# The last stage's adapters fetched by a register address in steps over six sequences, and the causal mask of two head groups by POOL

## The reference, cut to what matters

```python
# L1 attention, one of 4 layers; layer 0 is the same without rel
scores = (einsum('bhqd,bhkd->bhqk', q, k) + rel) * HEAD_DIM ** (-0.5)   # 16 heads of 8
mask = jnp.arange(S)[None, :] > jnp.arange(S)[:, None]
scores = jnp.where(mask[None, None], NEG, scores)
p = jax.nn.softmax(scores, axis=-1)
# L3_ffn: one adapter of eight for each sequence
base = jnp.einsum('btd,od->bto', x, base_W) + base_b
m1, m2 = x.mean(axis=1), (x * x).mean(axis=1)
losses = (m2 . inv_var - 2.0 * m1 . (disc_mu * inv_var) + sum(disc_mu ** 2 * inv_var)) / D
idx = jnp.argmin(losses, axis=0)
h = jax.nn.relu(x @ down_W[idx] + down_b[idx])
a = h @ up_W[idx] + up_b[idx]
return base + (a @ conv_W[idx].T + conv_b[idx])
```

## Time and profile before

| what | value |
|---|---|
| median of 3 runs | 7136.94 us (7130.81 to 7144.48) |
| the profiled execution's own time | 7138.57 us |
| its span in the trace | 7136.8 us |
| PE busy | 6011.8 us (84%) |
| DVE busy | 4420.2 us (62%) |
| ACT busy | 2803.8 us (39%) |
| POOL busy | 1534.3 us (21%) |

### The profile page before, as it was taken

The page is one execution under the profiler, slowest core; times in us unless marked ns, Lnnn a source line. Parts: engine busy times, 40 slices in busy tenths (PEclk is TensorE's granted clock), DMA queues, the critical chain, the costliest instruction groups (busy, mean ns, idle before and its releaser), DMA issues. The chain is left out here.

```text
span 7136.8 us, 123309 instructions
## 1 busy us (share of the span) xinstructions
PE 6011.8 (84%) x39533; PEld 3728.4 (52%) x39533; DVE 4420.2 (62%) x10235; ACT 2803.8 (39%) x4536; POOL 1534.3 (21%) x1885
## 2 busy tenths in 40 slices
PE   8997999999949998899879987998898987355455
PEld 5773444444426774577457754775454663234322
DVE  6764666666646763677356745774454666796565
ACT  4552222222214554355435543554444553123211
POOL 4320000000023331333133313331001224222100
PEclk9998999999969999999989998999888998678755
DMA  4333323223325540555045513552000000000000
GB/s 131 104 82 104 97 96 96 97 96 96 97 65 138 145 122 6 142 141 144 8 124 135 144 35 97 139 143 58 4 0 3 0 4 0 3 0 2 7 0 24
DMA packets 524294, 522.62 MB, mean 73 GB/s; under 512 B 56244, under 2 KB 434691, under 8 KB 501766
## 3 DMA queue, kind: packets, MB, share of 16 engines
q1 hardware_dynamic: 523990, 518.91, 26.2%
HBM read 333.65 MB, written 185.07 MB: 73 GB/s over the span
## 5 line engine op out<-in xcount | busy, mean ns | idle before, releaser
L346 DVE TENSOR_REDUCE a_mx<-a_unit 128x2 f32<-128x512 f32 (+1 forms) x1920 | 1305.0, 690 | 748.1 <-PE a_unit L522 737.9
L436 ACT ACTIVATE a_prob<-a_slot 128x1536 f32<-128x1536 f32 x640 | 928.4, 1451 | 853.3 <-PE a_slot L545 853.3
L520 PE MATMUL a_unit<-a_sk,a_sq 96*128 96x256 bf16 (+3 forms) x5120 | 752.0, 250 | 75.6 <-DMA a_sk<-a_kscratch 56.1
L1125 ACT ACTIVATE f_silu<-f_pG 128x512 f32<-128x512 f32 x528 | 314.8, 598 | 940.9 <-PE f_pG L1198 940.7
L1071 DVE TENSOR_TENSOR f_gated<-f_spread,f_silu 128x512 f32<-128x512 f32 x512 | 354.6, 693 | 403.8 <-ACT f_silu L1125 358.7
L522 PE MATMUL a_unit<-a_maskq,identb 128*128 128x256 bf16 (+1 forms) x1920 | 603.6, 314 | 0.0
L520 PEld LDWEIGHTS a_unit<-a_sk,a_sq 96*128 96x128 bf16 (+1 forms) x5120 | 399.8, 99 | 341.8 <-DVE a_mx L346 129.5
L1177 PE MATMUL f_pO<-f_hidden,f_wd 128*128 128x512 f32 x1056 | 547.1, 600 | 16.6 <-DVE f_hidden L1073 15.9
L1198 PE MATMUL f_pG<-f_xnT,f_wg 128*128 128x512 f32 x1056 | 542.7, 596 | 0.0
L1202 PE MATMUL f_pU<-f_xnT,f_wu 128*128 128x512 f32 x1056 | 541.0, 594 | 0.0
L538 PE MATMUL a_slot<-a_sq,a_sk 98*128 98x256 bf16 (+1 forms) x2560 | 463.1, 274 | 81.3 <-DMA a_sq<-a_mscratch 71.5
(11 more groups left out here) (411 smaller groups left out, 11509.8 us busy)
## 6 DMA issues: line engine op xcount, KB each, us to landing
f_spread<-f_scratch SPq DMA_DIRECT2D x1024, 128.0 KB, 2.9
a_sq<-a_qscratch SPq DMA_DIRECT2D x128, 768.0 KB, 5.7
a_sk<-a_kscratch SPq DMA_DIRECT2D x160, 384.0 KB, 6.7
a_qscratch<-a_parts SPq DMA_DIRECT2D x288, 192.0 KB, 2.2
a_qscratch<-a_parts SPq DMA_DIRECT2D x288, 128.0 KB, 2.2
a_kscratch<-a_parts SPq DMA_DIRECT2D x160, 192.0 KB, 2.2
a_kscratch<-a_parts SPq DMA_DIRECT2D x160, 128.0 KB, 2.1
a_qscratch<-a_parts SPq DMA_DIRECT2D x288, 64.0 KB, 1.8
```

Of the source, the lines that this page charges most:

```text
L346: v.tensor_reduce(dst, src, op=ALU.max, axis=AX.X, negate=True).then_inc(red_done, 1)
L436: act.activation(prob[gr % 2][:, :], slot[:, :], ACT.Exp, scale=SCALE).then_inc(exp_done, 1)
L520: pe.matmul(bank[:, at * wide:(at + 1) * wide], q, sk[b][0:KM, gr * GH + h, 0:wide], start=(at == 0), stop=False)
```

## The change

Two edits, in different stages.

*In the attention*, groups 0 and 1 of four (`SELECTED = 2`) leave out the three products with `maskk`. Instead POOL sets the exponentials to zero where a key lies behind its query, with two `affine_select` instructions on `prob` (128 x 512 float32 each) for each group. `values` of these groups waits for POOL (`sel_done`) instead of ACT. On POOL's queue group 0's pair stands ahead of 1/sqrt(var), group 1's behind it and ahead of the split of q and k.

*In the adapters*, the stage is written anew in the steps of `fours`: in step n, the stats are for sequence n+5, the normalised rows and their transpose for n+4, the losses and the choice for n+3, the first products for n+1, the last for n, the add to x for n-1. The choice is read into a register of SP, and one transfer fetches that adapter (128 x 323) from DRAM into one of four tiles. Mean and 1/std come from POOL in the steps, and there is no `row_moments`, no `every` and no `pB`. ACT sums both x and its square as it copies. `store_out` goes: SP stores each sequence two steps after its last products.

```diff
                 def step(i, j):
                     n = i * 4 + j
+                    def causal(gr):
+                        if not is_seq(n):
+                            return
+                        g.wait_ge(exp_done, n * GROUPS + gr + 1)
+                        g.sem_inc(apart, 1)
+                        wide = prob[gr % 2][:, 0:2 * BLK].rearrange("p (h q) -> p h q", q=SEQ)[:, :, 0:P]
+                        tail = prob[gr % 2][:, 2 * BLK:3 * BLK].rearrange("p (h q) -> p h q", q=P)
+                        g.affine_select(wide, wide, [[0, GH], [1, P]], ALU.is_ge, zero, base=0, channel_multiplier=-1)
+                        g.affine_select(tail, tail, [[0, GH], [1, P]], ALU.is_ge, zero, base=0, channel_multiplier=-1
+                                        ).then_inc(sel_done, 1)
                     if not rel and is_seq(n - 1):
 ...
                         g.tensor_tensor(guard[:, :, :], zeros[:, :, :], zeros[:, :, :], op=ALU.add).then_inc(guard_done, 1)
+                    causal(0)
                     if is_seq(n + 5):
                         g.wait_ge(stats_done, n + 6)
                         ln_rstd(g, chain, moments, veps, mhalf, rstd, eps, rstd_done, apart)
+                    causal(1)
 ...
-                            pe.matmul(bank.rearrange("p (h k) -> p h k", k=SEQ)[:, :, 0:P], identb,
-                                      maskk[:, :].unsqueeze(1).broadcast_to((P, 2, P)), start=False, stop=True)
+                            if gr >= SELECTED:
+                                pe.matmul(bank.rearrange("p (h k) -> p h k", k=SEQ)[:, :, 0:P], identb,
+                                          maskk[:, :].unsqueeze(1).broadcast_to((P, 2, P)), start=False, stop=True)
 ...
-                        pe.wait_ge(exp_done, m * GROUPS + gr + 1)
+                        if gr < SELECTED:
+                            pe.wait_ge(sel_done, m * SELECTED + gr + 1)
+                        else:
+                            pe.wait_ge(exp_done, m * GROUPS + gr + 1)
 ...
 # adapters: the queue of SP
+                    if is_seq(n + 3):
+                        b = (j + 3) % 4
+                        sp.wait_ge(picked, n + 4)
+                        choice = sp.value_load(at[b][0:1, 0:1], min_val=0, max_val=E - 1)
+                        if is_seq(n - 1):
+                            sp.wait_ge(yT_done, n)
+                        sp.dma_start(mine[b][:, :], w["every"][bass.ds(choice, 1), :, :].rearrange("e p c -> p (e c)")
+                                     ).then_inc(loaded[b], 16)
+                    if is_seq(n - 2):
+                        sp.wait_ge(x_done, n - 1)
+                        sp.dma_start(out[bass.ds(n - 2, 1), :, :].rearrange("s (t p) d -> p (s t) d", p=P),
+                                     rows(core["x"], (n - 2) * QT, QT)).then_inc(put, 16)
 ...
 # DVE
+                    if is_seq(n + 4):
+                        v.wait_ge(rstd_done, n + 5)
+                        ln_apply(v, rows(core["x"], (n + 4) * QT, QT), moments, rstd, xn).then_inc(xn_done, 1)
+                    if is_seq(n + 3):
+                        v.wait_ge(l_pe, n + 4)
+                        link(v.tensor_scalar(gain[:, :], pL[0:1, 0:E], -1.0 / (D * SEQ), None, ALU.mult))
+                        link(v.max(best[:, :], gain[:, :]))
+                        v.max_index(at[(j + 3) % 4][:, :], best[:, :], gain[:, :]).then_inc(picked, 1)
+                    if is_seq(n - 1):
+                        v.wait_ge(r_pe, n)
+                        v.tensor_tensor(dst, pR[:, 0:SEQ].rearrange("p (t d) -> p t d", d=D), dst, op=ALU.add
+                                        ).then_inc(x_done, 1)
+                    v.drain()
+                    if is_seq(n + 5):
+                        ln_stats(v, chain, rows(core["x"], (n + 5) * QT, QT), stats, moments, stats_done)
```

More of the change, by code:

```diff
@@ new lines, in adapters @@
+        stats = k.sb("stats", [P, QT, 6]); moments = k.sb("moments", [P, QT, 2])
+        veps = k.sb("veps", [P, QT]); rstd = k.sb("rstd", [P, QT])
+        xn = k.sb("xn", [P, QT, D]); xnT = [k.sb(f"xnT{b}", [P, SEQ]) for b in range(4)]; sqr = k.sb("sqr", [P, SEQ])
+        sum1 = k.sb("sum1", [P, 1]); sum2 = k.sb("sum2", [P, 1])
+        gain = k.sb("gain", [1, E]); best = k.sb("best", [1, E])
+        at = [k.sb(f"at{b}", [1, E], mybir.dt.uint32) for b in range(4)]
+        mine = [k.sb(f"mine{b}", [P, W]) for b in range(4)]; outb = [k.sb(f"outb{b}", [P, 1]) for b in range(4)]
@@ L2148, in adapters, with used @@
+        loaded = [k.sem(f"loaded{b}") for b in range(4)]
+        W_IN = 16 * 4
+        def used(i, j, ahead):
+            return 16 * i + ((j + ahead) // 4 + 1) * 16
         with nc.Block() as block:
@@ L2150, in _ @@
             def _(sp):
[L2151 to L2155, removed]
-                                 (sigma[:, :], w["sigma"]), (iota[:, :], core["iota8"])):
-                    sp.dma_start(dst, src).then_inc(w_in, 16)
+                for dst, src in ((mu, w["mu"]), (sigma, w["sigma"]), (base, w["base"]), (baseb, w["baseb"])):
+                    sp.dma_start(dst[:, :], src).then_inc(w_in, 16)
@@ L2159, in _ @@
+                fours(sp, step)
+                sp.wait_ge(x_done, SEQS)
+                sp.dma_start(out[SEQS - 1:SEQS, :, :].rearrange("s (t p) d -> p (s t) d", p=P),
+                             rows(core["x"], (SEQS - 1) * QT, QT)).then_inc(put, 16)
+                sp.wait_ge(put, 16 * SEQS)
             @block.gpsimd
             def _(g):
-                g.memset(every[:, :, :], 0.0).then_inc(setup, 1)
-                g.memset(biases[:, :, :], 0.0).then_inc(setup, 1)
-                g.memset(ones1[:, :], 1.0).then_inc(setup, 1)
@@ L2164, in _, with step @@
-                g.memset(onescol[:, :], 1.0).then_inc(setup, 1)
+                chain = Chain(g)
+                g.memset(length[:, :], float(SEQ)).then_inc(setup, 1)
+                chain.link(g.memset(mhalf[:, :], -0.5))
+                g.wait_ge(w_in, W_IN)
+                def step(i, j):
+                    n = i * 4 + j
+                    if is_seq(n + 1):
+                        b = (j + 1) % 4
+                        g.wait_ge(loaded[b], used(i, j, 1))
+                        if is_seq(n - 3):
+                            g.wait_ge(yT_done, n - 2)
+                        g.tensor_tensor(outb[b][:, :], mine[b][:, BC:BC + 1], baseb[:, :], op=ALU.add).then_inc(outb_done, 1)
+                    if is_seq(n + 5):
+                        g.wait_ge(stats_done, n + 6)
+                        ln_rstd(g, chain, moments, veps, mhalf, rstd, 1e-5, rstd_done, apart)
@@ L2166, in _ @@
+                fours(g, step)
             @block.vector
@@ L2234, in step @@
                                        ).then_inc(aT_done, 1)
-                        act.wait_ge(y_pe, n + 1)
-                        act.activation(yT[:, :], pY[:, 0:SEQ], ACT.Identity, bias=outb[:, 0:1]).then_inc(yT_done, 1)
-                rounds(act, step, SEQS)
+                fours(act, step)
             @block.tensor
@@ L2431, in twos @@
         step(n // 2, n % 2)
+SELECTED = 2
 def part_of(a, prefix):
@@ L2490, in load_core @@
     return core
-def store_out(nc, store, out):
-    put = nc.alloc_semaphore("out_written")
-    with nc.Block() as block:
-        @block.sync
-        def _(sp):
-            for c in range(8):
-                sp.dma_start(out.rearrange("s (t p) d -> p (s t) d", p=P)[:, c * 8:(c + 1) * 8, :],
-                             store[:, c * 8:(c + 1) * 8, :]).then_inc(put, 16)
-            sp.wait_ge(put, 128)
 def constants():
```

241 lines of the change are left out of this document (120 added, 121 removed).

## The result

| what | before | changed |
|---|---|---|
| median | 7136.94 us (7130.81 to 7144.48) | 6752.74 us (6751.02 to 6756.28, 4 runs) |
| span of the profiled execution | 7136.8 us | 6754.2 us |

The ratio is 0.9462 [0.9445, 0.9478]: 384 us less, where 321 were forecast.

The account below looks back on a forecast made before the run. Bounds: a chain through the pick in the adapters, PE in layer 0, a loop of two steps in L1. Savings 271 + 9 + 41 = 321 us from 7138.6, less 1.6 for the median: 6816 us, range 6765 to 6885.

Parts of the forecast that it names:

- The last stage: Adapters: DVE's loop with POOL bounds a step, taken as 4.8 us; stage 456 to 185 us, 271 less.
- the dear end: Adapters: upper bound of 5.9 us a step, with PE at the lower clock.
- The fetch: Adapters: three steps must hold 5 us and the fetch; even at 13.73 us, a step would be 6.2.
- Layer 0: Attention: PE saves 0.88 us a step, late transposes cost 0.6, leaving 0.28 a step, 9 us.
- the charge for DVE's standstill: L1: DVE standing still beside POOL's selects adds 0.25 us to the loop of two steps (bounds 0 and 0.8).
- The loop of two steps: L1: three legs sum to 33.67 us per two steps; only the first gains, 0.44 a step before the charge.
- The selects: POOL, attention: 0.61 us a select, 1.35 a pair with its gap, 2.47 kept for the range; nothing late at 1.35.
- all: Rival, attention: DVE gets ahead of POOL everywhere, masks bring 84 us, not 50; with adapters at 4.6, 6776; chance 0.13.
- The adapters did not stay at the lower clock: Denies a rival: adapters at lower clock or waiting for the fetch, 5.9 to 6.2 a step, 6862 us; chance 0.08.
- The masks bring nothing: Rival, attention: dear selects or L372 late; L1 gains 0.04, layer 0 loses 0.3; total 6871; chance 0.22.
- slower: Rival, attention: POOL becomes the limit if a select reaches 2.1 us; at 3 us, 7439 us; chance 0.05.

Follow-up runs that it names:

- e4: Changed kernel with DVE's stats of n+5 in the last stage moved right behind the normalised rows of n+4: 6738.4 us, ratio 0.945.
- e1: Changed kernel with all four groups masked by PE again, so the new adapters alone: 6822.3 us, ratio 0.956 to the kernel before.
- e9: Changed kernel without its selects, so groups 0 and 1 have no mask at all: 6760.2 us, ratio 0.9477.
- e3: Changed kernel with POOL's first pair of selects also waiting until DVE has split the negated maxima: 6744.1 us, ratio 0.9457.
- four masked kernels: The changed kernel and three runs with the same attention code in L1; L1 took 2671 us in their mean.
- e10: Changed kernel with all four groups left without mask, neither selects nor PE's masks: 6719.9 us, ratio 0.9421.
- e2: Kernel before with POOL's masks for two groups and the old adapters kept: 7064.7 us, ratio 0.9905.
- e6: Changed kernel with L1's row of maxima loaded ahead of the two stacks of q and k: 6749.3 us, ratio 0.9459.

## Why the prediction was right or wrong, step by step

- **The last stage: mechanism right, size wrong; this is the step that put the time outside the range.** The failed term is 31 x 4.8 = 149 us for the steps: it measured 113.8 from the first add to the last. A steady step took 3.96 us, which makes 26 of the 35 us; the other 9 are the last five steps, which take 1.9 to 2.6 us each and which the term counted as full. The filling with barrier and loads took 24.5 us in place of 32, the last store 4.6 in place of 4. That is 42 us together. By the two spans, which lie 383 us apart, 62 us were missed: these 42 and 29 of L1, less 3 of layer 0 and 6 of stages that no edit touches. The 4.8 was a value between 4.4, which is stage_a3's step and has more DVE work, and 5.9, PE at the lower clock. The loop itself is 2.65 us on DVE and 1.31 through POOL, and the second number was in the prediction (1.32); I took a neighbour's total in place of adding up the parts. And PE was granted 1.00 in all of the steps (the filling ahead of them had 0.58), so the dear end did not exist. The range allowed for nothing under 4.4 a step. e4 shows that the loop is the bound.
- **The fetch**: it landed 2.3 us after its issue (median of 27). No engine waited for it in the steady steps, as forecast; POOL's bias sum (`outb`) did so in three of the last steps, 6.6 us together.
- **Layer 0: the charge was right, the saving too large, and the total near by luck.** 0.88 saved less 0.6 for the late transposes was to give 0.28 a step, 9 us. The step went from 15.65 to 15.55 us, 0.10, and layer 0's own copies (first to last) lie 3 us closer. The stretch is 6.8 us shorter (the mean of before and e1 against four kernels with the changed attention) because 1.7 come from the filling of L1, which has masks too, and some 2 from the experts. The charge measured 0.59 in e9, and e3 names its place. But the saving was 0.69 and not 0.88: PE comes earlier to `maxima(2)` and now waits there for DVE's reduction of an earlier unit. From the first transpose of `xn` to that product lie 0.25 us before and 0.44 in the changed kernel, e3 and e9 (means of 16 steps). First before, then the changed kernel:
```profile
303.60 0.41 PE L588 MATMUL a_ring<-ident,a_xn 128*128 128x128 f32 x2
303.85 0.38 PE L520 MATMUL a_unit<-a_sk,a_sq 80*128 80x256 bf16 x2
```
```profile
304.51 0.69 DVE L362 TENSOR_REDUCE a_mx<-a_unit 128x4 f32<-128x512 f32 x1 [0.18 <-issue]
...
304.86 0.41 PE L611 MATMUL a_ring<-ident,a_xn 128*128 128x128 f32 x2
305.26 0.39 PE L536 MATMUL a_unit<-a_sk,a_sq 80*128 80x256 bf16 x2
```
- **L1: the charge for DVE's standstill was wrong.** I added 0.25 us to the loop of two steps, 16 us in all. The loop's first leg fell by 0.90, all of PE's masks, though L387 and L388 do stand still there too (0.71 and 0.54 us at 2393.07 and 2393.86, the first beside the split's L342, the second beside a select): the transposes came 3.54 us behind `scores(0)`, as they should without the masks, and their wait for DVE is 6.8 us over all of L1. e3, which removes the standstill beside the selects, leaves L1 as it was. Of the 28 us missed in L1 (by the means of above) the charge is 16. Another 9 are the last four steps of each layer: together they are 3.9 us shorter (52.4 us in the mean of before and e1, 48.5 in the four masked kernels, from copy to copy), where I had counted 0.44 each. The last 3 are the steady steps, with 0.47 in place of 0.44, which is within L1's scatter.
- **The loop of two steps: right as far as the change goes, wrong beyond it.** It forecast 0.44 a step and 0.47 came (16.93 us in the mean of before and e1, 16.46 in the four masked kernels, in the middle steps of all layers by the start of `scores(0)`). But its rule, half of PE's saving, fails in e10. No kernel here has L1 under 2659 us. That the clock is the cause of the 17 to 19 us by which e9 and e10 are longer is argued from the sums above and not shown by an experiment of its own: in e9 the shortfall behind the waits grew by 10 us only, in e10 by 61.
- **The selects**: 0.61 taken, 0.64 measured; a pair 1.23, where 1.35 was taken. By the branching rule that the prediction quoted from the Trainium skill (GPSIMD Engine Reference, "Elementwise — side-by-side cycle accounting") it would have been 5.1 us; the trace is on the side of that section's non-branching figure, 0.77. PE waited for POOL's selects 6.4 us in the whole kernel, in the short last steps.
- **The rivals.** The masks brought less than all in layer 0 and, in L1, all that the loop allows. The adapters did not stay at the lower clock. "The masks bring nothing" and "slower" fell with the select's price. Taken alone, e2's 67 us lie between the forecast 50 and the "all" of 84. Two sums are off by their own terms, and neither moved the forecast: the fixed part of the slower rival is 414 and not 403 (its threshold 4.3 us a pair, not 4.2), and 4.4 us a step makes 283 us less, or 286 with the filling, not 287.

## What to carry to other kernels

When a new stage's bound is a loop between engines, add up that loop from the rows of its own instructions; a neighbouring stage's step is a check on it, not a value for it. Count the last, emptier steps of a pipeline apart, and let the range reach below the sum as well as above. A saving on an engine that waits for a transfer in every second step was worth its share of the loop here (0.47 us of 0.88); what was taken from PE beyond that became idle time, behind which the granted clock fell more often, and the stage did not get shorter. Where the engine looks fully busy, a saving still need not count in full: 0.88 us gave 0.69, because PE then arrived ahead of DVE at another place. Where POOL is to take over work, put it behind the short DVE instructions for which PE waits: here that order alone made layer 0's stretch 14.5 us shorter.

## What the runs showed of the hardware

- DVE stands still beside POOL's `affine_select` not only with two SBUF inputs (L388, 0.19 to 0.52 us) but in a cast with one (L387, 0.17 to 0.54) and in L67's `TENSOR_SCALAR` of 128 x 128 float32 (two take 1.24 us beside two selects, 0.60 without). The rule that the prediction quoted from the Trainium skill (SBUF — State Buffer, "SBUF: two separate sides"), one shared pair of ports as an exclusive lock, agrees with this: each of the two short ones ended together with a select.
- Of three loads that are issued one behind the other (768, 384 and 16 KB) PE waited most for the one that came last in the queue. Moving the small one ahead moved the wait to the other (83.0 us for the row in the changed kernel, 109.5 us for the stack of k in e6) and gained nothing.
- PE's granted clock, at 1.00 in L1's steady steps of the changed kernel (2340 to 2520 us), fell behind some 2 us of idle time to a mean of 0.67 over the next 5.2 us at one place of e10, and stayed at 1.00 behind as long a wait at another, in the same kernel.
